# Copying the later batches' modulation behind the last modulated tile, with new orders of steps

## The reference: conditioned attention with a residual

```python
scale, shift = split(cond @ W_emb + b_emb, 2)            # one row per batch
xn = rms_norm(x) * g_norm * (1.0 + scale) + shift
q, k, v = (xn @ W_qkv) as 16 heads of 64
q, k = rms_norm(q) * g_q, rms_norm(k) * g_k
o = softmax(q @ k.T * 64 ** -0.5) @ v                    # per batch and head
out = x + o + o @ W_out
```

## Time and profile before

| | us |
|---|---|
| median of 3 runs | 2212.49 (2211.74 to 2212.57) |
| the profiled execution's own time | 2209.7 |
| its span | 2207.9 |
| PE busy in the span | 2158.0 (98%) |
| VectorE / ScalarE / GpSimd busy | 1623.6 / 1492.5 / 908.0 |

### The profile page before, as it was taken

The page is one execution under the profiler, slowest core; times in us unless marked ns, Lnnn a source line. Parts: engine busy times, 40 slices in busy tenths (PEclk is TensorE's granted clock), DMA queues, the critical chain, the costliest instruction groups (busy, mean ns, idle before and its releaser), DMA issues.

```text
span 2207.9 us, 39088 instructions
## 1 busy us (share of the span) xinstructions
PE 2158.0 (98%) x13392; PEld 1983.1 (90%) x13392; DVE 1623.6 (74%) x2999; ACT 1492.5 (68%) x3205; POOL 908.0 (41%) x1241
## 2 busy tenths in 40 slices
...
GB/s 320 243 281 257 163 220 229 247 290 226 207 191 218 299 209 170 241 219 263 206 189 236 238 247 200 160 260 278 216 202 173 242 281 224 204 192 229 266 184 96
DMA packets 141525, 497.53 MB, mean 225 GB/s; under 512 B 14864, under 2 KB 61968, under 8 KB 140304
## 3 DMA queue, kind: packets, MB, share of 16 engines
...
## 4 chain that ended last, share of the span: by engine, by line
PE 78%; ACT 6%; DVE 4%; issue 3%; POOL 1%; DMA 1%; ACTq 0%; SPq 0%; DVEq 0%; POOLq 0%
PE proj_bank L611 17%; PE proj_bank L613 17%; PE proj_bank L612 16%; PE flip_bank L736 8%; PE score_bank L727 5%; PE score_bank L728 4%; PE pv_bank L747 4%; PE pv_bank L748 4%; ACT k_hi L860 2%; PE score_bank L700 2%; PE flip_bank L707 1%; ACT probs L875 1%; DVE k_lo L1058 1%; DVE stage L986 1%; ACT pt_hi L885 1%
## 5 line engine op out<-in xcount | busy, mean ns | idle before, releaser
L611 PE MATMUL proj_bank<-w_ring,xa_hi 128*128 128x384 f32 x1792 | 626.4, 350 | 12.3 <-POOL xa_lo L1198 7.1
L613 PE MATMUL proj_bank<-w_ring,xa_lo 128*128 128x384 f32 x1792 | 605.4, 338 | 0.0
L612 PE MATMUL proj_bank<-w_ring,xa_hi 128*128 128x384 f32 x1792 | 604.5, 337 | 0.0
L875 ACT ACTIVATE probs<-score_bank,neg_max 128x512 f32<-128x512 f32 x512 | 352.8, 691 | 202.1 <-DVE neg_max L1088 168.4
L1099 DVE TENSOR_TENSOR pt_lo<-flip_bank,pt_hi 128x512 fp32r<-128x512 f32 x512 | 347.9, 685 | 173.1 <-ACT pt_hi L885 170.0
L885 ACT CAST pt_hi<-flip_bank 128x512 fp32r<-128x512 f32 x512 | 296.9, 588 | 230.5 <-PE flip_bank L736 170.0
L1088 DVE TENSOR_REDUCE neg_max<-score_bank 128x1 f32<-128x512 f32 x512 | 345.9, 685 | 82.4 <-PE score_bank L728 78.8
L611 PEld LDWEIGHTS proj_bank<-w_ring,xa_hi 128*128 128x128 f32 x1792 | 338.9, 189 | 37.1 <-issue 8.7
L612 PEld LDWEIGHTS proj_bank<-w_ring,xa_hi 128*128 128x128 f32 x1792 | 339.4, 189 | 11.4
L613 PEld LDWEIGHTS proj_bank<-w_ring,xa_lo 128*128 128x128 f32 x1792 | 338.2, 189 | 0.0
L1191 POOL TENSOR_TENSOR v_split<-stage,v_split 128x256 fp32r<-128x256 f32 x128 | 94.5, 740 | 512.0 <-ACT v_split L848 511.8
...
## 6 DMA issues: line engine op xcount, KB each, us to landing
...
```

Of the source, the lines that this page charges most:

```text
L611: nc.tensor.matmul(dst, a_hi, w[:, 0, :], start=start, stop=False, skip_group_check=shared)
L612: nc.tensor.matmul(dst, a_hi, w[:, 1, :], start=False, stop=False, skip_group_check=shared)
L613: return nc.tensor.matmul(dst, a_lo, w[:, 0, :], start=False, stop=stop, skip_group_check=shared)
L875: nc.scalar.activation(probs[h][:, i, :], score_bank[n % 2][:, :], ACT.Exp, bias=neg_max[:, n:n + 1], accum_out=row_sum[:, n:n + 1]).then_ ...
```

## The change

Two edits. The first moves the call of `save_mod()` on VectorE from behind X0 of the first batch to behind X6, which is the last half tile that VectorE modulates. The second writes the orders of the steps anew, in all three tables; the steps themselves are the same ones, and HEAD changes most. The start of TensorE's list in HEAD and of SyncE's in BODY stand here for all lists:

```diff
 HEAD = {
     "TensorE": """
-        Z0 X0 X4 X1 X5 X2 X3 0C0 0C1 0C2 X6 X7 0C3 0C4 0C5 0C6 0C7 0C8 0C9 0C10 0C11 0C12 0C13 0C14 0C15 0C16
+        Z0 X0 X4 X1 X5 X2 0C0 X3 0C1 X6 0C2 X7 0C3 0C4 0C5 0C6 0C7 0C8 0C9 0C10 0C11 0C12 0C13 0C14 0C15 0C16
...
     "SyncE": """
-        4W4 -O15 +X0 4W5 +X1 4W6 E0 +X2 4W7 4W8 +X3 E1 4W9 4W10 4W11 4W12 4W13 6W0 6W1 6W2 6W3 6W4 E2 6W5 E3 6W6
+        +X0 -O15 4W4 +X1 4W5 4W6 E0 +X2 4W7 4W8 +X3 4W9 4W10 4W11 4W12 4W13 6W0 6W1 6W2 6W3 E1 6W4 6W5 E2 E3 E4
...
                     elif kind == "X":
                         modulate(b + d, n)
-                        if is_first(b + d) and n == 0:
+                        if is_first(b + d) and n == 6:
                             save_mod()
```

More of the change, by code:

```diff
@@ L42 @@
[L42 to L51, removed]
@@ new lines @@
+    "GpSimd": """
+        0J0 0J1 0J2 X7 0L4 0J3 X11 0L5 X8 0L6 X12 X10 0L7 X9 0L8 0J4 0L9 0L10 0J5 0D0 0L11 0L12 0D1 0M0 0M1 0D2
+        0D3 0M2 0M3 X13 0L13 1D0 2L0 1D1 2L1 1M0 0V0 1D2 1M1 2L2 2J0 2L3 1D3 1M2 1M3 0V1 2J1 1V0 2J2 2J3 2L4 2L5
+        2L6 2L7 1V1 2J4 2D0 2L8 2L9 2D1 2L10 2J5 2L11 2M0 0Q0 2L12 2M1 2D2 2D3 2M2 2M3 2V0 2L13 4L0 4L1 3D0 3D1
+        3M0 2V1 4L2 3D2 3M1 3D3 4J0 3M2 4L3 3M3 4J1 +A0 1Q0 +A1 4L4 +A2 4J2 4L5 4L6 4J3 +A3 3V0 4L7 3V1 4L8 4J4
+        4L9 4L10 4J5 4L11 4D0 2Q0 4D1 4L12 4L13 4M0 4V0 4M1 4D2 4M2 4D3 4M3 6L0 6L1 6L2 5D0 6J0 6J1 6L3 4V1 5D1
+        6J2 6J3 5D2 5M0 6L4 6L5 5D3 5M1 5M2 5M3 +X7 6L6 6J4 6L7 6L8 6L9 6D0 6D1 6M0 5V0 3Q0 5V1 6M1 6J5 +X8 +X1
+        6L10 4Q0 6L11 6L12 +X0 +X4 6L13 +X3 6D2 6D3 6M2 6M3 +X11 7D0 +X5 7M0 7D1 6V0 +X12 7D2 +X10 6V1 7D3 7M1
+        7M2 7M3 +X9 +X13 +X6 +X2 7V0 5Q0 7V1 8D0 8D1 8D2 8M0 6Q0 8M1 8D3 L0 8M2 8M3 L1 L2 8V0 9D0 L3 7Q0 9M0 8V1
+        9D1 L4 9D2 9D3 9M1 L5 L6 L7 9M2 9M3 9V0 9V1 10D0 10D1 10D2 10M0 10M1 10D3 10M2 10M3 L8 11D0 11M0 L9 L10
+        L11 L12 11D1 11M1 11D2 11D3 L13 11M2 11M3 L14 10V0 L15 10V1""".split(),
@@ L121 @@
+        O12 O13 12W2 O14 12W3""".split(),
 }
@@ L169 @@
-    "GpSimd": """
-        0Q0 1Q0 +A0 3V0 3V1 4D0 4D1 +A1 2Q0 4M0 4M1 4D2 +A2 4D3 4M2 4M3 5D0 4V0 4V1 +A3 +X0 5D1 5M0 5M1 5D2 5M2
-        3Q0 5D3 5M3 5V0 +X7 6D0 5V1 6M0 +X1 6D1 +X8 6M1 4Q0 +X4 +X11 6D2 6M2 6D3 6M3 7D0 +X5 6V0 +X10 7D1 7M0
-        7M1 +X3 7D2 6V1 +X9 7D3 7M2 7M3 +X12 5Q0 +X2 7V0 7V1 8D0 8D1 8M0 8M1 8D2 6Q0 8M2 8D3 8M3 +X6 +X13 7Q0
-        9D0 8V0 9D1 9M0 9M1 9D2 9M2 9D3 9M3 8V1 9V0 9V1 10D0 10D1 10D2 10M0 10M1 10M2 10D3 10M3 11D0 11D1 11D2
-        11M0 11M1 10V0 11M2 11D3 11M3 10V1""".split(),
@@ L175 @@
[L175 to L180 removed]
+        4C0 4C1 4C2 2W0 2W1 4C3 4C4 2W2 2F4 4C5 2F5 2W3 4C6 2F6 2W4 2W5 2F7 4C7 2W6 4C8 3F0 3S6 2W7 3S7 4C9 3F1
@@ new lines @@
+    "GpSimd": """
+        0Q0 1Q0 3V0 +A0 3V1 4D0 2Q0 +A1 4D1 +A2 4M0 +A3 4M1 4D2 4D3 4M2 4M3 5D0 4V0 5M0 5D1 +X0 5D2 3Q0 4V1 5M1
+        5M2 5D3 5M3 5V0 6D0 +X7 5V1 +X1 6M0 6D1 4Q0 6M1 +X8 +X4 +X11 6D2 6D3 6M2 6M3 7D0 +X5 6V0 7M0 +X10 7D1
+        +X3 7D2 7M1 +X9 6V1 7D3 +X12 7M2 7M3 +X2 5Q0 7V0 7V1 8D0 8D1 8M0 8M1 6Q0 8D2 8M2 8D3 8M3 +X6 8V0 +X13
+        9D0 7Q0 9D1 9M0 9D2 9M1 9M2 9D3 9M3 8V1 9V0 9V1 10D0 10D1 10M0 10M1 10D2 10M2 10D3 10M3 11D0 11D1 11M0
+        11D2 11M1 11M2 11D3 11M3 10V0 10V1""".split(),
```

285 lines of the change are left out of this document (141 added, 144 removed).

## The result

The changed kernel takes 2214.53 us (median of 19 runs), the kernel before 2211.2 us in as many runs beside it. The ratio of the two is 1.0015, with a 95% interval from 1.0008 to 1.0022: 3.3 us slower (1.8 to 4.9), where 2.5 us faster was forecast. The median lies inside the predicted range, the direction is wrong. (The kernel before stands at 2211.2 us in these 19 runs, 1.3 us under the median of three runs from which the forecast of 2210.0 was reckoned.) One of the changed kernel's 19 runs took 4047 us at a mean granted clock of 0.87, and the ratio leaves it out. The profiled execution of the changed kernel took 2214.65 us, its span is 2212.9 us.

The account below looks back on a forecast made before the run. PE is busy 2158.0 of 2207.9 us, bound by its own rate in later batches and by what feeds it in the first; -1.1 - 1.4 + 0 = -2.5 us from 2212.49 gives 2210.0, range 2204.3 to 2215.8.

Parts of the forecast that it names:

- 335 us to the end: Middle batches and most of the last: same steps at PE's rate, value 0, bounds -3 and +4 us.
- Rival (c): Six middle batches: weight load 4W4 comes late behind store O15 and a load of x; slower, 2218.6 us, chance 0.11.
- Z0 to 0T0, -1.1: First batch's start: 0C6 0.5 us earlier, 0C10 0.3, 0T0 1.1 us earlier after one GpSimd split fewer.
- Rival (b): Start's lead lost: 0J1, 0J2 run against GpSimd, 0C6 and 0C10 as before, DVE-bound stretch gives nothing; 2212.5 us, chance 0.21.
- the rule quoted: VectorE instructions with two SBUF inputs and GpSimd share a locked port pair; by it 0C6 gains nothing instead of 0.5 us.
- The late save_mod "at nothing": First batch, save_mod ahead of G4: G4 0.4 us later, over 4 us of cover before Y12, cost nothing, at most 1.79 us.
- 92.4 to 335 us, -1.4: Rest of first batch's feeding-bound stretch: 0.5 us at 2S0 and one probability wait of 0.9 us go, -1.4 us.
- The idle time forecast, 18 to 20 us: Sign: PE's idle time from 92.4 to 335 us should be 18 to 20 us.
- The chance of 0.12 for slower: Whole kernel above 2216.9 us: rival (c) and a little of rival (b)'s edge.

Follow-up runs that it names:

- e12: Changed kernel with store O0 and load E4 ahead of H4, E7 ahead of O4 (SyncE), and 10S1 ahead of L12 (ScalarE): 2211.26 us, ratio 1.0003.
- e7: Changed kernel with the remainder Y2 on VectorE moved ahead of G5 instead of behind 0D0: 2214.58 us, ratio 1.0015.
- e3: Kernel before with the first template's new orders up to about 330 us and save_mod behind X6: 2211.28 us, ratio 1.0003.
- e11: Kernel before with e3's first template, the new middle table with 4D2 and 4D3 moved ahead, and the new last table: 2208.62 us, ratio 0.9989.
- e6: Kernel before with only the last batch's table new: 2208.66 us, ratio 0.9989.

## Why the prediction was wrong

**The step that failed** is "335 us to the end": "The same steps at PE's rate", value 0. It measured +4.7 us in the trace (3.1 + 2.8 - 1.2), past its own bound of +4, and PE's idle time there grew by 3.7 us where under 2 was the sign. The reasoning was that PE is never short of work there, since it waits 8.4 us in 1873. But that was how the old lists were laid, with each product ready just in time. The rows of PE's waits tell how well the lists fit, not how much room there is between them: 4M3 ended 0.64 us before 4T0 in the kernel before (488.36 against 489.00), 9T1 0.18 us before 9S0 (367.85 against 368.03). A new order of the same steps can use up such margins anywhere in 1873 us, and it was not followed there at all.

One pair of profiles has its own chances in it. The sixteen profiles taken together have each stretch several times with the old lists and with the new ones without their mends. These are the means in us, with the ranges and the number of profiles:

| stretch | old list | new list | difference |
|---|---|---|---|
| Z0 to 0T0 | 50.1 (48.9 to 50.9; 4) | 51.4 (49.1 to 54.4; 8) | +1.3 |
| 0T0 to P0 | 256.0 (254.8 to 257.7; 6) | 254.3 (253.1 to 256.0; 9) | -1.6 |
| P0 to 4C0 | 108.8 (108.5 to 109.2; 8) | 111.6 (111.0 to 112.7; 4) | +2.8 |
| six middle batches | 1585.8 (1585.3 to 1586.4; 6) | 1587.5 (1587.0 to 1588.0; 5) | +1.7 |
| last batch | 169.4 (169.1 to 169.7; 6) | 168.2 (167.6 to 168.6; 10) | -1.2 |

In the last three stretches the ranges don't touch. From P0 on this is +3.3 us, from Z0 to the end +3.0, against 3.3 measured: the term that had 0 is the whole loss, and the middle table's part in it is smaller than the 2.8 us of one pair.

**Rival (c)** had the right sign, the right part of the program (six middle batches) and the wrong mechanism. 4W4 behind O15 costs nothing: PE's waits for DMA are 1.0 us before and after. Its kind, a transfer held up by those moved ahead of it in SyncE's list, did strike, once and elsewhere: O0 and E4 behind H4 and G8 at the end of the first template.

**Z0 to 0T0, -1.1.** It measured -0.7 in the pair of profiles (49.8 to 49.1 us), with 0C6 at 58.58 and 0C10 at 69.06 where 57.4 and 68.3 were forecast. X4 came right behind X0 and 0C0 at 44.69, with Z0 0.66 us late, so this much held. But X2 ran at 47.8 to 47.9 in four profiles with its list (Z0 at 37.1 to 37.3) and at 48.95 to 49.15 in four others (Z0 at 35.8 to 36.6). Rival (b), which had 0.21 as a whole, says in its first half that the J steps run against GpSimd and 0C6 and 0C10 start as before, and this was the better forecast. Of the rule quoted (the Trainium skill, SBUF — State Buffer, "SBUF: two separate sides": an exclusive lock, held for the whole instruction) the traces show the effect, 0.55 or 1.2 to 1.6 us for the same instruction; which of the two it is went with 1 us of Z0's start. Where the text weighed it, only 0J2 was priced as long (0.7 us). In e12 0J1 and Y1 were long too, 2.9 and 1.5 us where 1.8 and 0.6 were taken, so X2 ended at 50.4 instead of 48.0, and the chain over X6 and 0C2, which the text had right, carried this on.

**The late save_mod "at nothing"** was right in its result and wrong in its readers. G4 started at 57.18, 1.9 us later than before and not 0.4 (the text ends X2 at 48.0 in one place and at 48.3 in another; it ended at 49.1). G4's readers were looked at, not what stands behind on VectorE: Y2, and PE's 0C8 with 4.15 us. e7 shows that 0C10 behind it takes this all back.

**92.4 to 335 us, -1.4.** From 0T0 to P0 the profile has 255.4 us before and 255.5 after, as if nothing had been won. But e3 and e11, with the same lists, have 253.1 and 253.5, and the means above have -1.6. So this term was about right, and what hides it in the one pair goes with the granted clock (last section). The idle time forecast, 18 to 20 us, was 17.3.

**The last batch** was inside the same 0 and won 1.2 us in the trace, 2.4 in e6's median.

The chance of 0.12 for slower had one mechanism in it. Three engines' margins in two tables were open besides, and following what each of PE's steps in a middle batch waits for through the new lists would have shown 4C19 closer to 4T0, with 4E9, 4D2 and 4M3 in a row between them.
